# Giving out a pair's 25 row scatters five at a time, the last five one pass later

## The reference

```python
x = x + conv_block(ln_channels(x))       # sign, 3x3 conv, BN, PReLU, sign, 1x1 conv, BN, PReLU
t = to_tokens(x)
h = ln_tokens(t)
e = argmax(h @ gate_w + gate_b)          # one of 8 networks for a token
pos = rank of the token within its network; kept = pos < capacity
t = t + where(kept, prob * (relu(h @ w1[e] + b1[e]) @ w2[e] + b2[e]), 0)
out = from_tokens(t)
```

## Time and profile before

| what | value |
|---|---|
| time, median of 3 runs (lowest to highest) | 1895.83 us (1888.43 to 1896.14) |
| span of the profiled execution | 2079.0 us |
| PE busy, instructions | 1654.2 us (80%), 10341 |
| DVE busy, instructions | 1482.2 us (71%), 3641 |
| ACT busy, instructions | 1206.3 us (58%), 4066 |
| POOL busy, instructions | 1048.5 us (50%), 1052 |
| scatters L490 | 400, 435.4 us busy |
| adds L484 | 112, 137.0 us busy |

### The profile page before, as it was taken

How to read it: one execution, slowest core, us unless ns; L and a number is a source line. 1 busy time by engine, 2 the same in 40 slices (tenths; PEclk the granted TensorE clock), 3 DMA queues, 4 the chain that set the end, 5 groups by cost and what they waited for, 6 DMA issues and landing times.

```text
span 2079.0 us, 40865 instructions
## 1 busy us (share of the span) xinstructions
PE 1654.2 (80%) x10341; PEld 880.9 (42%) x10341; DVE 1482.2 (71%) x3641; ACT 1206.3 (58%) x4066; POOL 1048.5 (50%) x1052
## 2 busy tenths in 40 slices
PE   7998888888888878775058888888888888878884
PEld 1344433443333434443034444555555445445453
DVE  3488878878887878888135666787677777777675
ACT  3687877777777877765035554655455454455451
POOL 2116655655676656667524444554444444444442
PEclk7898989988899989886579999999999999999896
DMA  9136766554557554442164555777777677777786
GB/s 240 40 97 145 176 165 157 150 142 117 148 149 135 139 133 108 108 112 78 59 191 142 145 147 144 193 219 244 226 234 230 220 236 225 228 222 228 227 247 221
DMA packets 302207, 351.64 MB, mean 169 GB/s; under 512 B 48452, under 2 KB 252452, under 8 KB 295940
## 3 DMA queue, kind: packets, MB, share of 16 engines
q1 hardware_dynamic: 260644, 264.23, 47.2%
q0 software_dynamic: 41120, 85.81, 13.3%
q10 hardware_dynamic: 320, 0.33, 0.1%
HBM read 179.70 MB, written 180.01 MB: 173 GB/s over the span
## 4 chain that ended last, share of the span: by engine, by line
PE 37%; issue 16%; DVE 14%; another core or an unknown queue 11%; POOL 8%; ACT 6%; DMA 4%; SPq 2%; ACTq 1%; POOLq 0%; DVEq 0%
PE bank L821 9%; PE bank L831 8%; POOL pairs_by_group L490 6%; PE bank L812 3%; PE bank L730 3%; POOL X L484 3%; PE bank L692 2%; PE bank L839 2%; PE bank L789 2%; PE bank L740 2%; DMA X<-weights_by_group 2%; PE bank L763 2%; ACT X L975 2%; DVE Z L1250 1%
## 5 line engine op out<-in xcount | busy, mean ns | idle before, releaser
L521 POOL DMA_INDIRECT results_by_pair<-X,PAIRNO x462 | 461.2, 998 | 542.1 <-ACT X L980 420.6
L490 POOL DMA_INDIRECT pairs_by_group<-ROWS,idx x400 | 435.4, 1088 | 133.2 <-issue 113.9
L821 PE MATMUL bank<-X 64*128 64x256 f32 x1848 | 287.7, 432 | 60.6 <-issue 28.7
L975 ACT ACTIVATE X<-bank,X 128x256 f32<-128x256 f32 x693 | 284.6, 474 | 76.2 <-PE bank L821 58.9
L968 ACT ACTIVATE X<-bank 128x256 f32<-128x256 f32 x231 | 90.5, 392 | 389.9 <-remote 238.1
L484 POOL TENSOR_TENSOR X<-Z,X 128x448 f32 (+1 forms) x112 | 137.0, 1223 | 308.9 <-DVE Z L1266 290.9
L831 PE MATMUL bank<-X 128*64 128x256 f32 x1848 | 276.3, 424 | 6.9 <-ACT X L985 6.9
L812 PE MATMUL bank<-ident,X 128*64 128x128 f32 x1848 | 159.3, 294 | 145.5 <-DMA X<-weights_by_group 69.2
L821 PEld LDWEIGHTS bank<-X 64*128 64x128 f32 x1848 | 180.3, 200 | 114.7 <-issue 103.3
L730 PE MATMUL bank<-S,WB 128*128 128x448 bf16 x1008 | 227.9, 374 | 0.0
L1289 DVE TENSOR_SCALAR X<-bank,X 128x256 f32<-128x256 f32 x231 | 111.1, 481 | 131.8 <-PE bank L821 63.3
(11 more groups left out here) (209 smaller groups left out, 3006.5 us busy)
## 6 DMA issues: line engine op xcount, KB each, us to landing
X<-weights_by_group SPq DMA_DIRECT2D x231, 258.5 KB
X<-pairs_by_group SPq DMA_DIRECT2D x231, 134.0 KB
pairs_by_group<-PAD SPq DMA_DIRECT2D x15, 1742.0 KB
X<-in_x_dram SPq DMA_DIRECT2D x16, 1568.0 KB
block_output<-X SPq DMA_DIRECT2D x112, 224.0 KB, 1.9
ROWS<-block_output SPq DMA_DIRECT2D x16, 1568.0 KB
Z<-results_by_pair SPq DMA_DIRECT2D x16, 1568.0 KB
out_dram<-ROWS SPq DMA_DIRECT2D x16, 1568.0 KB
```

Source lines behind the costliest of these rows:

```text
L490: pool.indirect_dma_start(rows, bass.IndirectOffsetOnAxis(ap=idx[0:m, p.odd, k:k + 1], axis=0), ROWS[0:m, p.odd, k, :], None).then_inc(s_s ...
L521: pool.indirect_dma_start(done, bass.IndirectOffsetOnAxis(ap=PAIRNO[:, u, j:j + 1], axis=0), RES[:, u, j, :], None,).then_inc(s_back[u], 16)
L821: mm(hidden(q), WR[b, ring, q // 2 * P:(q // 2 + 1) * P], XT[b, ring % 2, :], start=True, stop=True).then_inc(s_h, 1)
L975: last = A(HB[:, ring % 2, q, :], hidden(q), ACT.Relu, bias=WR[:, ring, at:at + 1])
```

## The change

POOL gives out a pair's 25 scatters in other places. Before, chunks 1 to 6 of a pass gave out 4, 4, 4, 4, 4 and 5. Now chunks 1 to 4 give out 5 each, chunks 5 and 6 none, and the last five follow in chunk 0 of the next pass, ahead of add 6. One more pass at the end gives out the last five of the last pair. Nothing else is changed; line numbers are one higher from L79 on and three higher behind the loop of POOL.

```diff
+    SCATTER_AT = (0, 5, 10, 15, 20)
...
-            def one_pass(con, rou, sca):
+            def one_pass(con, rou, sca, end):
                 for c in range(NCH):
                     late, j = (con, c - 1) if c else (rou, NCH - 1)
-                    if sca and c:
+                    if end and c == 0:
+                        scatter_tiles(end, SCATTER_AT[4], TILES)
+                    if sca and 1 <= c <= 4:
                         if c == 1:
                             wait_apart(pool, s_rr, sca.n + 1)
                             wait_apart(pool, s_rw, sca.n + 1)
                             wait_apart(pool, s_pad, sca.n * 16 + 16)
-                        scatter_tiles(sca, (c - 1) * TILES // (NCH - 1), c * TILES // (NCH - 1))
+                        scatter_tiles(sca, SCATTER_AT[c - 1], SCATTER_AT[c])
                     if late:
                         add_block(late, j)
...
-                one_pass(pick(0), pick(-1), pick(-2))
+                one_pass(pick(0), pick(-1), pick(-2), pick(-3))
...
-            for i in range(PAIRS, PAIRS + 2):
+            for i in range(PAIRS, PAIRS + 3):
                 run(i, i % 2)
```

## The result

The changed kernel takes 1974.31 us (median of 4 runs, 1965.43 to 1980.48) against 1895.55 us before (4 runs, 1888.43 to 1896.14): a ratio of 1.039 [1.035 to 1.043]. The forecast was 45 us more, 1940 us; slower was right, the size was too small: 1974.31 lies above the forecast's own range (1917 to 1957), where rival C was put (1961 to 1979), and the wide range (to 1975) holds it by less than a microsecond.

The account below looks back on a forecast made before the run. POOL's stretch from add 6 to add 3 was taken to bound each pass's first 30.5 us, a PE and DVE chain the rest. 13 passes x 3.8 = 49, x 0.912 = 45 us: 1896 + 45 = 1941, forecast 1940 (1917 to 1957).

Parts of the forecast that it names:

- rival C: Full 5.1 us in every pass, 1961 us, plus PE's half clock behind group 3's wait, 1979 us at most; chance 0.27.
- the wide range: The forecast's range of 8 in 10, from 1892 up to 1975 us.
- Add 3 ends 5.1 us later: POOL, chunks 1 to 4: four more scatters, 3 x 1.29 + 1.75 = 5.6 us, of which idle gaps may hide 0.5.
- In the other five PE's own lateness hides a part: Group 3 in five of ten passes: 2.5 us of the delay arrives instead of 5.1; mean over both kinds 3.8 a pass.
- the delay goes into the chain: PE behind group 3: routing sums and chunk 6 hand the 3.8 us a pass on to the next add 6.
- The factor of 0.912: Scaled recorded time to run time, the recorded execution being 1.097 times the median run: 49 us became 45.
- The edits at nothing: No scatters in chunks 5 and 6, five in chunk 0, and ACT's wait for those: each taken as 0 us.
- Chunks 5 and 6: Add 5 on POOL loses its lateness, worth 0 to 2.4 us in such a pass, off the chain; taken as 0.
- The five in chunk 0: Ahead of add 6: 6.5 us of scatters lie in POOL's 11.08 us wait for DVE and cost nothing.
- rival D: ACT's copies of groups 6 to 8 wait for chunk 0's scatters: 1966 us at 2 us beyond the slack; chance 0.05.
- Rival A: Faster: POOL has room, DVE holds chunks 2 to 4, and chunks 5 and 6 gain: 1884 us; chance 0.12.

Follow-up runs that it names:

- e0: The kernel before, unchanged, recorded once more: run 1918.71 us, span 1916.8; 19 runs of it on that chip had a median of 1906.69 us.
- e1: Against the kernel before, only the last five scatters moved, from chunk 6 to chunk 0 of the next pass: 1902.01 us, ratio 0.9996.
- e3: Changed kernel with three scatters in each of chunks 1 to 4, four in 5 and 6, five in chunk 0: 1909.51 us, ratio 1.0008 to before.
- e2: Changed kernel with the last five scatters in chunk 5, none in the next pass: 1960.92 us, ratio 1.032 to the kernel before.
- e4: Changed kernel with six scatters in each of chunks 1 to 4, the last one in chunk 0: 2043.64 us, ratio 1.069 to the kernel before.
- e5: Changed kernel with four scatters in each of chunks 1 to 3, eight in chunk 4, five in chunk 0: 1988.67 us, ratio 1.0405 to before.
- e6: Changed kernel with eight scatters in chunk 1, four in 2, 3 and 5, none in 4 and 6, five in chunk 0: 1973.07 us, ratio 1.0322.
- e7: The changed kernel again, no edit: 1966.6 us, ratio 1.0291 to the kernel before.
- e10: The changed kernel a third time, no edit, beside e8: 1964.97 us, ratio 1.0294 to the kernel before.
- e8: Changed kernel plus eight extra matmuls on PE ahead of group 3's wait for add 3: 1951.1 us, ratio 1.0224 to the kernel before.

## Why the prediction was right and wrong

**The place and the sign were right.** The stretch of POOL from add 6 to add 3 sets the start of group 3, PE hands the delay on, and nothing pays it back: from the convolution of chunk 6 to add 6 it takes 19.65 us against 19.75 in e0. Every experiment that leaves the adds where they were is level with before (e1, e3), and every one that makes an add later is slower (e2, e4, e5, e6). That the wide range reached 1974.31 us, by 0.7 us, is luck; by the ratios of e7 and e10 the time would be 1951 us, inside the forecast's own range.

**"Add 3 ends 5.1 us later": it was 4.0** (34.9 - 30.9). The scatters were priced nearly rightly: in the pass shown, chunk 4's five take 8.94 us from 682.64 to the add at 691.58, so 1.9 us more than four did (1.75 counted). From add 6 to add 2 it is 23.55 us (657.78 to 681.33) against 19.82 (633.43 to 653.25), 3.7 us more, and 4.1 with the 0.33 us of idle time that is gone, where 3 x 1.29 = 3.9 was counted. What was missed is add 3 itself. In the earlier trace rows it took 2.06 us, now 1.14: 0.9 us less in such a pass. On the mean over e0 and after it got 0.7 us shorter, and the idle time ahead of adds 2 and 3 that went was 0.9 us, not 0.5: 5.6 - 0.7 - 0.9 = 4.0.
The Trainium skill, "SBUF — State Buffer", section "Who interferes with whom", would, by its sentence on descriptors, have had the five at the plain spacing beside DVE's `TENSOR_TENSOR`s; here they took 1.39, 1.80, 1.14, 1.53 and 1.83 us, so the trace stays against it.

**"In the other five PE's own lateness hides a part": 0.6 us a pass, not 1.3.** The five late passes of the earlier trace rows belong to the disturbed record (one, pair 7's, was 3.75 us late, more than the 3.4 counted, and of the five direct ones PE stood idle in three only); in e0 two of ten are late at group 3, by 0.7 us on the mean over all. In after it is 0.1. Late passes turn into direct ones, as rival C said. These two misses nearly cancel, which is luck: 4.0 - 0.6 = 3.4 us a pass, where the forecast had 3.8.

**PE's clock was taken as nothing, and was the term that failed.** The step that failed is "the delay goes into the chain": the forecast moved the work behind group 3 at its old price, and gave the half clock to rival C alone, at 1.4 us a pass. It measured 1.8 us (6.41 - 4.6), and 2.1 in the repeats. Sum: 3.4 + 1.8 = 5.2 us a pass, which is what the pass grew (61.07 - 55.91 = 5.16). PE's waits for adds grew as much (7.56 - 2.30), but that is no second proof: its waits for ACT fell, so that all its idle time grew by 2.5 us a pass and its busy time, at the lower clock, by 2.7. Ten passes make 52 of the 61 us of the two records; those of pairs 2 and 3 add 11.7 and those of 14 and 15 2.7, and the first two and the end give 5 back. e8 gives 2.1 of the clock's part back in the rows. The prediction's own sign for C, passes longer by 5 us and more with PE's clock lower, is what the records show once e0 stands for before.
The Trainium skill, "TensorE: Matmul & The Clock Gate", section "HAM oscillation — how this bites in real kernels", has a wait that comes back in every round drop the clock each time; the rows agree for most rounds: in eight of after's ten passes group 3's wait was 1.58 to 3.92 us and the granted clock behind it 0.50 to 0.70, in the other two, after 0.28 and 0.41 us, it stayed at 1.00, as it did in nine of e8's ten, where PE was given work ahead of it. By that rule the forecast would have been nearer to rival C.

**The factor of 0.912** came from taking the first record's length as the price of recording. A record's span is within 3 us of its run, in after as in e0; without the factor the forecast's 49 us would have stood.

**The edits at nothing held.** Chunks 5 and 6: add 5 now waits 8.56 us for DVE, so it is no longer POOL's, and the pass gained nothing from it. The five in chunk 0: e1, level; the wait ahead of add 6 shrank from 10.80 us in e0's pass to 2.58, as cover does. ACT's new wait (rival D): the copies of the groups of chunk 0's tiles never waited in after; all that ACT waited for scatters in 610 us is this, from the view of waits of after (total us, times, longest):

```profile
ACT ROWS L951 <- DMA pairs_by_group<-ROWS,idx: 6.7, 6, 2.2
```

**Rival A** was right that DVE holds chunks 2 to 4 (e0's adds 2 and 3, and e3), and wrong on what follows: it holds them at a tie, so POOL had no room for the five more.

## What to carry to other kernels

Where two engines reach a place at the same moment, work put on either side costs in full and work taken from one side gains nothing; a few tenths of idle time ahead of a step, where others of its kind have none, is the sign of such a tie, and the end of the other engine's step beside it settles it. Price a new wait of TensorE with the clock behind it: read the same work at both levels from the trace, and take the slow price if the wait is to come back in every pass. And compare the span of a record with the runs before reading slack from it: one that is 8% longer than the longest run is not the program at another scale.

## What the runs showed of the hardware

- One recorded execution of the same program took 2079.0 us, with the expert stage 127 us longer at a DMA share of 0.69 in place of 0.79, though runs lie between 1888 and 1929 us. What disturbed it is not known.
- Add 3 on POOL took 2.06 to 2.22 us in most passes of e0, e3 and e6; in the passes shown here it started beside two steps of DVE on the rows. In nine of after's ten passes it took 1.13 to 1.15 us; in the one below it came behind them: being late made it cheaper. e0's add at 590.26 and after's at 691.58 stand beside these two rows of DVE:

```profile
589.91 1.54 DVE L1212 TENSOR_TENSOR ROWS<-ROWS,rst 128x640 f32<-128x640 f32 x2
```

```profile
689.16 1.54 DVE L1215 TENSOR_TENSOR ROWS<-ROWS,rst 128x640 f32<-128x640 f32 x2
```

  The first ends at 591.45, 1.2 us into the add, the second at 690.70, before it. That the overlap is the cause was not tried by itself.
- Eight matmuls whose results nobody reads, ahead of the wait for POOL, kept TensorE at 2.4 GHz (granted clock 1.00) behind it in nine of ten passes and made what stood there 2.1 us shorter on the mean (e8 against e10).
